# A selective scan and sixteen experts in one kernel: the fourth state block's input product moves to GpSimd

## The chip, the cores and the metric

One core of a Trainium2 chip runs the whole program. The metric is the device time in microseconds from launch to end, and of several executions the median is given. The core has five engines with queues of their own: TensorE (PE; its weight loads are shown as PEld), VectorE (DVE), ScalarE (ACT), GpSimd (POOL) and SyncE (SP), which here only issues DMAs. They wait for one another by counting semaphores.

## The reference, cut to what matters

8 sequences of 1024 tokens, 256 features, all in fp32. A Mamba layer stands between layer norms, and behind it a layer of 16 experts, of which each token uses 4. Only the scan matters for the change:

```python
dt = softplus(dt @ dt_proj_w + dt_proj_b)            # tokens x 512 channels
dA = exp(dt[..., None] * A)                          # x 16 states
dBx = dt[..., None] * Bm[:, :, None, :] * xc[..., None]
h = dA_t * h + dBx_t                                 # along the tokens
y_t = einsum('bds,bs->bd', h, C_t)
y = (y + xc * D) * silu(z) @ out_proj_w + residual
# then layer norm, routing, and for each token
y = sum over experts of weight * (silu(g) * u) @ down_proj
```

## The kernel before

The 8192 tokens are cut into 16 chunks of 512 (`CH`), two to a sequence. A chunk with an odd number carries its first states on from the chunk before (`carry`), an even one starts from zero. 512 channels times 16 states are 64 rows of 128 partitions for each chunk; four such rows are a group, so a chunk has 16 groups (`GPC`) and the program 256 (`NGRP`). A group is one third of the ring `hs` (`NH = 3`), a tile of 128 partitions by four state blocks (`NBETA`, `beta`) of 512 tokens.

A pass p of the schedule has 16 turns g, one for each group G = 16 p + g of chunk p. In the same turns TensorE and ScalarE prepare chunk p + 1 (the projections, the convolution, z, dt: the functions `f_...`), chunk p − 1 is closed and routed (`p_...`), and the experts of the chunk before run, one expert each turn, ten turns late (`MOFF`). Passes 0 and the greater part of 1 have no expert work. In pass 15 no next chunk is left. Each engine's program is written by hand as a loop over all turns, and its order in a turn is the order of the calls; nothing reorders it.

What happens to a group:

- VectorE forms dx times B for group G + 1 at the end of turn G (`inputs`, line 858): one instruction over all four blocks, 2048 columns. It waits for the loads of dx and B and, by `s_y`, for TensorE to be done with group G − 2, which used the same third of the ring.
- ScalarE forms exp(A dt) block by block into two PSUM banks (`decay`, line 501), waiting for the scan before the last.
- VectorE scans the four blocks in turn G (`scan`, line 872), each from its decays in PSUM and its inputs in `hs`. Around the first scan stand two products for an expert (lines 987 and 992).
- GpSimd waits until VectorE has formed the inputs of group G (`s_u`), weighs one expert's activations (`weigh`, line 751), and multiplies group G − 1 by C, all 2048 columns in one instruction (`read_out`, line 761).
- TensorE sums group G − 2 over its states into the bank Y (`add_states`, line 446) as the first thing of its turn G, then multiplies the expert's gate and up weights (416, 424), then the projections of that turn (343, 353, 379 and others), then the down weights of an older expert (434).
- VectorE multiplies Y by silu(z) in every fourth turn (`y_out`, line 879).

Between the fourth scan and the inputs VectorE has the work of a particular turn: the convolution's taps in turns 2 and 3 (line 831), Newton steps for the norms in turns 4, 6 and 12 (lines 788 to 817, opened by `tensor_scalar` at 801 or 810), the routing in turn 9 (924 to 983), the product for dx in turn 10 (847), residual sums in turns 5 and 13 (891, 1003). SyncE issues every load; those of dx and B wait by `s_u` until their buffer's last reader is done.

Of the kernel before, what the change touches and what calls it, by code (L numbers as in the profile page):

```python
# [6 lines left out]
ALU = mybir.AluOpType  # L7
ACT = mybir.ActivationFunctionType
AX = mybir.AxisListType
P = 128  # L10
# [3 lines left out]
CH = 512  # L14
TB = CH // P
KM = DM // P
MT = DI // P
# [4 lines left out]
NSIG = NS // SG  # L22
NBETA = P // CB
GPC = MT * NSIG
NGRP = NC * GPC
HIST = TAPS - 1
NH, NTH, NWD = (3, 3, 4)
# [43 lines left out]
def sandwich_kernel(nc, x, w_in, w_out, w_gu, w_dn, w_x, w_rt, cols, alog, ebias, consts, sel_dt, out):  # L71
    with ExitStack() as ctx:

        def sb(name, shape, dt=F32):
            return ctx.enter_context(nc.sbuf_tensor(name, shape, dt))
# [4 lines left out]
        def sem(name):  # L80
            return ctx.enter_context(nc.semaphore(name))
# [53 lines left out]
        dxr = sb('dxr', [P, 2, NBETA, CH])  # L135
        Bb = sb('Bb', [P, NSIG, CH])
        Cb = sb('Cb', [P, NSIG, CH])
        hs = sb('hs', [P, NH, NBETA, CH])
# [25 lines left out]
        f_act = Steps(sem('f_act'), ['xT0', 'xT1', 'raw0', 'tap0', 'raw1', 'tap1', 'raw2', 'tap2', 'raw3', 'tap3', 'z0', 'silu_x', 'xd', 'dt', 'z1', 'z2', 'z3', 'silu_z'])  # L164
        f_dve = Steps(sem('f_dve'), [f'c{k}{m}' for m in DVE_CONV for k in range(HIST)] + ['hist', 'dx'])
        fp_full = sem('fp_full')
        s_u, s_dA, s_h, s_keep, s_c, s_y, y_gate = (sem(k) for k in ('s_u', 's_dA', 's_h', 's_keep', 's_c', 's_y', 'y_gate'))
        route = ['den', 'score', 'sfc', 'ps', 't1', 't2', 'gs', 'ggt', 'geq', 'gq', 'ga', 'gr', 'gm', 'tmp', 'top', 'gt', 'eq', 'ng', 'cs', 'cn', 'ok', 'sel', 'w', 'ws', 'we', 'wr', 'comb']
        p_dve = Steps(sem('p_dve'), ['w1', 'nb', 'x1', 'Bw1'] + rsqrt_names('q') + ['Bnb'] + route)
        p_act = Steps(sem('p_act'), ['xn0', 'xn1', 'rev0', 'rev1', 'nm', 'sq', 'ro', 'sum2', 'nm2', 'sq2', 'x2', 'x2T0', 'x2T1', 'sig', 'cmT'])  # L170
# [7 lines left out]
        ld_dx = [sem(f'ld_dx{k}') for k in range(4)]  # L178
        ld_B = [sem(f'ld_B{s}') for s in range(NSIG)]
# [12 lines left out]
        def expert_at(G):  # L192
            q = G - GPC - MOFF
            return q if 0 <= q < NC * NE else None

        def groups():
            for p in range(-2, NC + 2):
                for g in range(GPC):
                    yield (p, g, p * GPC + g)

        @block.sync
        def _(sp):
# [18 lines left out]
            def load_dx(M, k):  # L221
                if M % MT == 0:
                    sp.wait_ge(st_dx, 16 * (M // MT + 1))
                if M >= 2:
                    sp.wait_ge(s_u, (M - 1) * NSIG)
                src = dx_d.rearrange('(M c k b) t -> M k c (b t)', k=2, b=2, c=CB)[M, k]
                sp.dma_start(dxr[:, M % 2, 2 * k:2 * k + 2, :].rearrange('p b t -> p (b t)'), src.unsqueeze(1).broadcast_to([CB, SG, 2 * CH])).then_inc(ld_dx[2 * (M % 2) + k], 16)

            def load_B(c, s):
                if s == 0:  # L230
                    sp.wait_ge(st_xd, 16 * (c + 1))
                if c > 0:
                    sp.wait_ge(s_u, c * GPC - NSIG + s + 1)
                src = bc_d.rearrange('(c k s g) t -> c k s g t', c=NC, k=2, s=NSIG)[c, 0, s]
                sp.dma_start(Bb[:, s, :], src.unsqueeze(0).broadcast_to([CB, SG, CH])).then_inc(ld_B[s], 16)

# [18 lines left out]
            for p, g, G in groups():  # L255
                c = p + 1
# [19 lines left out]
                if 0 <= p < NC:  # L276
                    M = p * MT
                    if g in (4, 8):
                        load_dt(M + g // NSIG + 1)
                        load_dx(M + g // NSIG + 1, 0)  # L280
                        load_dx(M + g // NSIG + 1, 1)
                    if g in (0, 1):
                        load_C(p, g + 2)
                if in_f(p) and g >= 12:
                    load_B(c, g - 12)
# [5 lines left out]
                if in_f(p) and g == 13:  # L291
                    load_dt(c * MT)
                    load_dx(c * MT, 0)
                    load_dx(c * MT, 1)
# [450 lines left out]
        @block.gpsimd  # L745
        def _(pool):

            def weigh(q):
                pool.wait_ge(m_w, q + 1)
                pool.wait_ge(ld_cm[q % 2], 16 * (q // 2 + 1))  # L750
                pool.tensor_tensor(th[:, q % NTH, :], th[:, q % NTH, :], cmb[:, q % 2, :], ALU.mult).then_inc(m_a, 1)  # L751

            def read_out(G):
                c, m, s = (G // GPC, G // NSIG % MT, G % NSIG)
                if m == 0:
                    pool.wait_ge(ld_C[s], 16 * (c + 1))
                if c % HALVES < HALVES - 1:
                    pool.wait_ge(s_keep, c // HALVES * GPC + G % GPC + 1)
                else:
                    pool.wait_ge(s_h, (G + 1) * NBETA)  # L760
                pool.tensor_tensor(hs[:, G % NH, :, :], hs[:, G % NH, :, :], Cb[:, s, :].unsqueeze(1).broadcast_to([P, NBETA, CH]), ALU.mult).then_inc(s_c, 1)  # L761
            for p, g, G in groups():
                if 0 <= G < NGRP:
                    pool.wait_ge(s_u, G + 1)
                q = expert_at(G - 2)
                if q is not None:
                    weigh(q)
                if 0 <= G - 1 < NGRP:
                    read_out(G - 1)

        @block.vector
        def _(dve):
# [76 lines left out]
            def inputs(G):  # L849
                c, M, s = (G // GPC, G // NSIG, G % NSIG)  # L850
                if s == 0:
                    for k in range(2):
                        dve.wait_ge(ld_dx[2 * (M % 2) + k], 16 * (M // 2 + 1))
                if M % MT == 0:
                    dve.wait_ge(ld_B[s], 16 * (c + 1))
                if G >= NH:
                    dve.wait_ge(s_y, G - NH + 1)
                dve.tensor_tensor(hs[:, G % NH, :, :], dxr[:, M % 2, :, :], Bb[:, s, :].unsqueeze(1).broadcast_to([P, NBETA, CH]), ALU.mult).then_inc(s_u, 1)  # L858

            def scan(G, beta):  # L860
                c, h = (G // GPC, G * NBETA + beta)
                k = G % GPC * NBETA + beta
                if beta == 0:
                    dve.wait_ge(s_u, G + 1)
                first = 0.0
                if c % HALVES:
                    if beta == 0:
                        dve.wait_ge(s_keep, c // HALVES * GPC + G % GPC + 1)
                    first = carry[:, k:k + 1]
                dve.wait_ge(s_dA, h + 1)  # L870
                hv = hs[:, G % NH, beta, :]
                dve.tensor_tensor_scan(hv, dA[h % 2][:, :], hv, first, ALU.mult, ALU.add).then_inc(s_h, 1)  # L872
# [131 lines left out]
            for p, g, G in groups():  # L1004
# [5 lines left out]
                if S:  # L1010
                    scan(G, 0)
                if q is not None:
                    expert_up(q)
                if S:
                    for beta in range(1, NBETA):
                        scan(G, beta)
# [35 lines left out]
                if 0 <= G + 1 < NGRP:  # L1052
                    inputs(G + 1)
# [34 lines left out]
```

## Time and profile before

| | |
|---|---|
| median of 3 runs | 2793.53 us (2791.71 to 2795.12) |
| the profiled execution | its span is 2792.0 us, and no time of its own beside it is given |
| VectorE busy | 2455.6 us, 88% of the span |
| TensorE busy (matmul) | 2414.2 us, 86% |
| ScalarE busy | 1628.2 us, 58% |
| GpSimd busy | 1474.8 us, 53% |
| DMA | 121 GB/s on the mean |
| mean granted TensorE clock | 0.953 of full speed |

The busy shares say how full an engine is over the whole span, not whether it sets the end. In the chain that ended last, TensorE has 42% of the span and VectorE 39%. A row of the timeline is one instruction, or a few like ones merged (xN), with start, duration, engine, line, output and inputs, and in brackets how long the engine stood idle before it and what released it. A matmul's end is modelled; GpSimd's times are rough.

### The profile page before, as it was taken

To read this page: it belongs to the slowest core of one execution; us is meant where nothing else is said; L and a number is where in the kernel's file an instruction comes from. 1 tells how busy PE (TensorE), PEld (TensorE's weight loads), DVE (VectorE), ACT (ScalarE), POOL (GpSimd) and SP (SyncE) were. 2 spreads that over 40 slices of the span, in tenths; PEclk is the share of its full clock that TensorE was granted. 3 is DMA by queue.
4 is the path that set the end of the run, shared out by engine and by line. 5 is a ranking of instruction groups with operands and counts; after the bars stand their busy time and mean duration, and the time that the engine had idled before them with its cause. 6 is when DMAs were issued, how large, how long until landed. Compare 5 with 4: busy or idle time off the path is not lost.

```text
span 2792.0 us, 27042 instructions
## 1 busy us (share of the span) xinstructions
PE 2414.2 (86%) x8416; PEld 1179.1 (42%) x8416; DVE 2455.6 (88%) x3265; ACT 1628.2 (58%) x3312; POOL 1474.8 (53%) x516
## 2 busy tenths in 40 slices
PE   4556799898989989899998989899898989988898
PEld 1112254443534444354444435354444445444454
DVE  1799998989899998989989898999989899899642
ACT  3566565666666566665666656665666665654331
POOL 0355564646556564655555465565646556565511
PEclk9677899999999999999999999999999999999999
DMA  1532332425244252524435252433525233352221
GB/s 36 226 107 90 129 139 96 160 94 177 77 144 140 98 170 81 188 74 143 133 105 172 79 184 83 136 130 105 179 79 175 95 124 128 100 177 70 64 76 59
DMA packets 164811, 336.65 MB, mean 121 GB/s; under 512 B 15771, under 2 KB 73404, under 8 KB 156220
## 3 DMA queue, kind: packets, MB, share of 16 engines
q1 hardware_dynamic: 164668, 334.93, 35.8%
q8 instruction: 67, 1.10, 0.2%
q14 instruction: 76, 0.62, 0.1%
HBM read 291.35 MB, written 43.52 MB: 120 GB/s over the span
## 4 chain that ended last, share of the span: by engine, by line
PE 42%; DVE 39%; issue 10%; ACT 9%; DMA 0%; SPq 0%; DVEq 0%; ACTq 0%
DVE hs L872 17%; DVE hs L858 9%; PE Gp L416 8%; PE Up L424 7%; PE MY L434 7%; PE FP L343 5%; PE FP L353 4%; PE FP L379 3%; PE Y L446 3%; DVE th L987 3%; DVE th L992 3%; PE FP L361 1%; ACT XC L571 1%; ACT XB L519 1%; ACT DX L636 1%
## 5 line engine op out<-in xcount | busy, mean ns | idle before, releaser
L761 POOL TENSOR_TENSOR hs<-hs,Cb 128x2048 f32<-128x2048 f32 x256 | 1159.1, 4528 | 203.7 <-DVE hs L858 203.7
L501 ACT ACTIVATE dA<-dtr,A 128x512 f32<-128x512 f32 x1024 | 699.7, 689 | 771.3 <-DVE hs L872 768.7
L751 POOL TENSOR_TENSOR th<-th,cmb 128x512 f32<-128x512 f32 x256 | 325.4, 1271 | 1096.8 <-DVE hs L858 980.7
L872 DVE TENSOR_TENSOR_SCAN hs<-dA,carry,hs 128x512 f32<-128x512 f32 x512 | 627.2, 1264 | 31.7 <-ACT dA L501 31.4
L416 PE MATMUL Gp<-x2T,Wgu 128*128 128x512 f32 x1024 | 530.4, 642 | 129.2 <-DVE th L987 129.0
L872 DVE TENSOR_TENSOR_SCAN hs<-dA,hs 128x512 f32<-128x512 f32 x512 | 596.2, 1203 | 50.6 <-ACT dA L501 50.1
L858 DVE TENSOR_TENSOR hs<-dxr,Bb 128x2048 f32<-128x2048 f32 x256 | 586.6, 2292 | 13.4 <-DMA dxr<-dx_d 12.3
L434 PE MATMUL MY<-Wdn,th 128*128 128x256 f32 x2048 | 486.3, 380 | 0.0
L424 PE MATMUL Up<-x2T,Wgu 128*128 128x512 f32 x1024 | 486.2, 597 | 0.0
L434 PEld LDWEIGHTS MY<-Wdn,th 128*128 128x128 f32 x2048 | 383.6, 190 | 136.5 <-issue 84.6
L416 PEld LDWEIGHTS Gp<-x2T,Wgu 128*128 128x128 f32 x1024 | 183.6, 198 | 473.4 <-issue 259.1
L446 PE MATMUL Y<-hs,Cst 128*32 128x512 f32 x2048 | 291.0, 642 | 21.5 <-POOL hs L761 21.5
L343 PE MATMUL FP<-xT,Win 128*128 128x512 f32 x512 | 262.1, 636 | 49.6 <-ACT SZ L565 15.8
L424 PEld LDWEIGHTS Up<-x2T,Wgu 128*128 128x128 f32 x1024 | 190.7, 192 | 260.8 <-issue 208.4
L987 DVE SCALAR_TENSOR_TENSOR th<-th,Gp 128x512 f32<-128x512 f32 x256 | 173.5, 678 | 68.1 <-ACT th L507 68.1
L507 ACT ACTIVATE th<-Gp 128x512 f32<-128x512 f32 x256 | 149.0, 582 | 114.8 <-PE Gp L416 114.8
L992 DVE TENSOR_TENSOR th<-Up,th 128x512 f32<-128x512 f32 x256 | 170.0, 664 | 10.0 <-PE Up L424 9.3
L343 PEld LDWEIGHTS FP<-xT,Win 128*128 128x128 f32 x512 | 95.8, 199 | 193.9 <-issue 94.5
L353 PE MATMUL FP<-XB,Kdiag 128*128 128x512 f32 x256 | 121.6, 620 | 11.6 <-ACT XB L551 11.6
L379 PE MATMUL FP<-Wout,SZ 128*128 128x256 f32 x512 | 122.6, 383 | 3.1 <-ACT DX L611 3.1
L379 PEld LDWEIGHTS FP<-Wout,SZ 128*128 128x128 f32 x512 | 98.0, 192 | 31.2 <-issue 14.3
L446 PEld LDWEIGHTS Y<-hs,Cst 128*32 128x32 f32 x2048 | 41.2, 110 | 149.5 <-issue 109.0
(131 smaller groups left out, 1827.1 us busy)
## 6 DMA issues: line engine op xcount, KB each, us to landing
dtr<-dt_d SPq DMA_DIRECT2D x64, 1024.0 KB, 5.5
dxr<-dx_d SPq DMA_DIRECT2D x128, 512.0 KB, 7.2
cmb<-cm_d SPq DMA_DIRECT2D x256, 256.0 KB, 3.6
Wdn<-in_w_dn SPq DMA_DIRECT2D x256, 128.0 KB, 3.5
dt_d<-XB SPq DMA_DIRECT2D x16, 1024.0 KB, 4.3
dx_d<-DX SPq DMA_DIRECT2D x16, 1024.0 KB, 5.8
Bb<-bc_d SPq DMA_DIRECT2D x64, 256.0 KB, 3.1
Cb<-bc_d SPq DMA_DIRECT2D x64, 256.0 KB, 4.0
```

Source lines behind the costliest of these rows:

```text
L343: mm = pe.matmul(FP[:, :], Win[:, q, c0:c0 + P], xT[:, q, :], start=q == 0, stop=q == KM - 1)
L379: pe.matmul(o, SZ[:, c % 2, m, b * P:(b + 1) * P], Wout[:, m, :], start=m == 0, stop=False)
L416: mm = pe.matmul(Gp[:, :], Wgu[:, k, e, 0:DE], x2T[:, c % 2, k, :], start=k == 0, stop=k == KM - 1)
L424: mm = pe.matmul(Up[:, :], Wgu[:, k, e, DE:2 * DE], x2T[:, c % 2, k, :], start=k == 0, stop=k == KM - 1)
L434: mm = pe.matmul(MY[b // 2][:, (b % 2) * DM:(b % 2 + 1) * DM], th[:, q % NTH, b * P:(b + 1) * P], Wdn[:, q % NWD, :], start=e == 0 and b % ...
L446: mm = pe.matmul(Y[beta * CB:(beta + 1) * CB, :], sel_y, hs[:, G % NH, beta, :], start=False, stop=s == NSIG - 1, tile_position=(0, beta * ...
L501: act.activation(dA[h % 2][:, :], dtr[:, M % 2, beta, :], ACT.Exp, scale=A[:, k:k + 1]).then_inc(s_dA, 1)
L751: pool.tensor_tensor(th[:, q % NTH, :], th[:, q % NTH, :], cmb[:, q % 2, :], ALU.mult).then_inc(m_a, 1)
L761: pool.tensor_tensor(hs[:, G % NH, :, :], hs[:, G % NH, :, :], Cb[:, s, :].unsqueeze(1).broadcast_to([P, NBETA, CH]), ALU.mult).then_inc(s ...
L858: dve.tensor_tensor(hs[:, G % NH, :, :], dxr[:, M % 2, :, :], Bb[:, s, :].unsqueeze(1).broadcast_to([P, NBETA, CH]), ALU.mult).then_inc(s_ ...
L872: dve.tensor_tensor_scan(hv, dA[h % 2][:, :], hv, first, ALU.mult, ALU.add).then_inc(s_h, 1)
L987: dve.scalar_tensor_tensor(out=th[:, q % NTH, :], in0=th[:, q % NTH, :], scalar=1.0, in1=Gp[:, :], op0=ALU.add, op1=ALU.mult).then_inc(m_v, 1)
```

## The change

GpSimd forms the input product of the fourth block (`last_input`), 512 columns, and VectorE's `inputs` keeps the other three, 1536 columns. GpSimd's product stands between `weigh` and `read_out` of a turn and is that of group G + 1. It carries its own semaphore, `s_u3`: the fourth scan waits for it, and SyncE's loads of dx and B wait for both counts.

```diff
@@ SyncE: load_dx and load_B
                     sp.wait_ge(s_u, (M - 1) * NSIG)
+                    sp.wait_ge(s_u3, (M - 1) * NSIG)
...
                     sp.wait_ge(s_u, c * GPC - NSIG + s + 1)
+                    sp.wait_ge(s_u3, c * GPC - NSIG + s + 1)
@@ GpSimd
+            def last_input(G):
+                c, M, s = (G // GPC, G // NSIG, G % NSIG)
+                if s == 0:
+                    pool.wait_ge(ld_dx[2 * (M % 2) + 1], 16 * (M // 2 + 1))
+                if M % MT == 0:
+                    pool.wait_ge(ld_B[s], 16 * (c + 1))
+                if G >= NH:
+                    pool.wait_ge(s_y, G - NH + 1)
+                pool.tensor_tensor(hs[:, G % NH, NBETA - 1, :], dxr[:, M % 2, NBETA - 1, :], Bb[:, s, :], ALU.mult).then_inc(s_u3, 1)
...
                 if q is not None:
                     weigh(q)
+                if 0 <= G + 1 < NGRP:
+                    last_input(G + 1)
                 if 0 <= G - 1 < NGRP:
                     read_out(G - 1)
@@ VectorE: inputs
-                dve.tensor_tensor(hs[:, G % NH, :, :], dxr[:, M % 2, :, :], Bb[:, s, :].unsqueeze(1).broadcast_to([P, NBETA, CH]), ALU.mult).then_inc(s_u, 1)
+                dve.tensor_tensor(hs[:, G % NH, 0:NBETA - 1, :], dxr[:, M % 2, 0:NBETA - 1, :], Bb[:, s, :].unsqueeze(1).broadcast_to([P, NBETA - 1, CH]), ALU.mult).then_inc(s_u, 1)
@@ VectorE: scan
+                if beta == NBETA - 1:
+                    dve.wait_ge(s_u3, G + 1)
```

GpSimd's queue in the middle of the program, before (three turns; `th` are an expert's activations, `cmb` its weights, `hs` the states):

```order
L751 TENSOR_TENSOR th<-th,cmb 128x512 [waits ld_cm0,m_w,s_u]
L761 TENSOR_TENSOR hs<-hs,Cb 128x2048 [waits s_keep]
L751 TENSOR_TENSOR th<-th,cmb 128x512 [waits ld_cm1,m_w,s_u]
L761 TENSOR_TENSOR hs<-hs,Cb 128x2048 [waits s_keep]
L751 TENSOR_TENSOR th<-th,cmb 128x512 [waits ld_cm0,m_w,s_u]
```

And now (`dxr` is dx, `Bb` is B):

```order
L753 TENSOR_TENSOR th<-th,cmb 128x512 [waits ld_cm0,m_w,s_u]
L763 TENSOR_TENSOR hs<-dxr,Bb 128x512 [waits s_y]
L773 TENSOR_TENSOR hs<-hs,Cb 128x2048 [waits s_h]
L753 TENSOR_TENSOR th<-th,cmb 128x512 [waits ld_cm1,m_w,s_u]
L763 TENSOR_TENSOR hs<-dxr,Bb 128x512 [waits s_y,ld_B0,ld_dx1]
L773 TENSOR_TENSOR hs<-hs,Cb 128x2048 [waits s_h]
```

A third instruction stands in each turn, with a wait for TensorE (`s_y`) in front of the read-out. VectorE's queue in turn 2 of a pass, before:

```order
L987 SCALAR_TENSOR_TENSOR th<-th,Gp 128x512 [waits m_th]
L872 SCALAR_TENSOR_TENSOR hs<-dA0,carry,hs 128x512 [waits s_dA,s_keep,s_u]
L992 TENSOR_TENSOR th<-Up,th 128x512 [waits m_v,m_u]
L872 SCALAR_TENSOR_TENSOR hs<-dA1,carry,hs 128x512 [waits s_dA]
L872 SCALAR_TENSOR_TENSOR hs<-dA0,carry,hs 128x512 [waits s_dA]
L872 SCALAR_TENSOR_TENSOR hs<-dA1,carry,hs 128x512 [waits s_dA]
L831 SCALAR_TENSOR_TENSOR XC<-XB,Cols,XC 128x512 [waits f_dve,f_act]
L831 SCALAR_TENSOR_TENSOR XC<-XB,Cols,XC 128x512 [waits f_dve] x2
L858 TENSOR_TENSOR hs<-dxr,Bb 128x2048 [waits s_y,ld_B3]
```

And the same turn now, from its third scan on:

```order
L888 SCALAR_TENSOR_TENSOR hs<-dA0,carry,hs 128x512 [waits s_dA]
L888 SCALAR_TENSOR_TENSOR hs<-dA1,carry,hs 128x512 [waits s_dA,s_u3]
L845 SCALAR_TENSOR_TENSOR XC<-XB,Cols,XC 128x512 [waits f_dve,f_act]
L845 SCALAR_TENSOR_TENSOR XC<-XB,Cols,XC 128x512 [waits f_dve] x2
L872 TENSOR_TENSOR hs<-dxr,Bb 128x1536 [waits s_y,ld_B3]
```

No instruction of VectorE changes its place; the last one is shorter and the fourth scan has one wait more.

## Rows read from the trace of the kernel before

**Rows 1.** The page's busy time: engine, us (share of the span), instructions.
```profile
PE 2414.2 (86%) x8416; PEld 1179.1 (42%) x8416; DVE 2455.6 (88%) x3265; ACT 1628.2 (58%) x3312; POOL 1474.8 (53%) x516
```

**Rows 2.** Timeline, VectorE and GpSimd in a short turn: start us, us, engine, line, operation.
```profile
1318.18 2.28 DVE L858 TENSOR_TENSOR hs<-dxr,Bb 128x2048 f32<-128x2048 f32 x1
...
1320.54 1.27 POOL L751 TENSOR_TENSOR th<-th,cmb 128x512 f32<-128x512 f32 x1 [4.08 <-DVE hs L858]
...
1321.76 4.52 POOL L761 TENSOR_TENSOR hs<-hs,Cb 128x2048 f32<-128x2048 f32 x1
...
1322.75 3.62 DVE L872 TENSOR_TENSOR_SCAN hs<-dA,carry,hs 128x512 f32<-128x512 f32 x3
...
1326.29 2.26 DVE L858 TENSOR_TENSOR hs<-dxr,Bb 128x2048 f32<-128x2048 f32 x1
```

**Rows 3.** Timeline, VectorE instructions alone and beside one of GpSimd.
```profile
1337.96 4.52 POOL L761 TENSOR_TENSOR hs<-hs,Cb 128x2048 f32<-128x2048 f32 x1
...
1342.25 2.38 DVE L858 TENSOR_TENSOR hs<-dxr,Bb 128x2048 f32<-128x2048 f32 x1
...
1554.66 1.21 DVE L891 TENSOR_TENSOR x<-DX,x 128x1024 f32<-128x1024 f32 x1
...
1699.01 4.54 POOL L761 TENSOR_TENSOR hs<-hs,Cb 128x2048 f32<-128x2048 f32 x1
...
1703.29 0.27 DVE L810 TENSOR_SCALAR ep_w<-e_s 128x4 f32<-128x4 f32 x1
...
2657.18 1.26 POOL L751 TENSOR_TENSOR th<-th,cmb 128x512 f32<-128x512 f32 x1 [9.59 <-DVE th L992]
2657.85 1.68 DVE L891 TENSOR_TENSOR x<-DX,x 128x1024 f32<-128x1024 f32 x1 [0.75 <-ACT DX L629]
```

**Rows 4.** Timeline of VectorE, the input products that open turns of pass 9.
```profile
1512.77 2.27 DVE L858 TENSOR_TENSOR hs<-dxr,Bb 128x2048 f32<-128x2048 f32 x1
...
1523.09 2.28 DVE L858 TENSOR_TENSOR hs<-dxr,Bb 128x2048 f32<-128x2048 f32 x1
...
1555.79 2.28 DVE L858 TENSOR_TENSOR hs<-dxr,Bb 128x2048 f32<-128x2048 f32 x1
...
1566.73 2.28 DVE L858 TENSOR_TENSOR hs<-dxr,Bb 128x2048 f32<-128x2048 f32 x1
...
1587.52 2.26 DVE L858 TENSOR_TENSOR hs<-dxr,Bb 128x2048 f32<-128x2048 f32 x1
...
1602.94 2.28 DVE L858 TENSOR_TENSOR hs<-dxr,Bb 128x2048 f32<-128x2048 f32 x1
```

**Rows 5.** Timeline of TensorE, the sums into Y in turns 2, 5, 6 and 9.
```profile
1517.48 1.07 PE L446 MATMUL Y<-hs,Cst 128*32 128x512 f32 x8
...
1550.33 1.06 PE L446 MATMUL Y<-hs,Cst 128*32 128x512 f32 x8
...
1562.69 1.06 PE L446 MATMUL Y<-hs,Cst 128*32 128x512 f32 x8
...
1594.96 1.06 PE L446 MATMUL Y<-hs,Cst 128*32 128x512 f32 x8
```

**Rows 6.** Timeline, VectorE in turn 7; ScalarE and TensorE in a turn 4.
```profile
1576.97 2.46 DVE L872 TENSOR_TENSOR_SCAN hs<-dA,carry,hs 128x512 f32<-128x512 f32 x2 [4.39 <-ACT dA L501]
...
1707.73 0.60 ACT L551 ACTIVATE XB<-FP 128x512 f32<-128x512 f32 x1 [0.62 <-PE FP L343]
...
1709.04 0.41 PEld L353 LDWEIGHTS FP<-XB,Kdiag 128*128 128x128 f32 x2
```

**Rows 7.** Timeline of TensorE in a turn 8, and its stretch (PEclk is the granted clock).
```profile
1421.37 3.18 PE L416 MATMUL Gp<-x2T,Wgu 128*128 128x512 f32 x4
...
1434.36 1.98 PE L416 MATMUL Gp<-x2T,Wgu 128*128 128x512 f32 x4
...
1420.00:1430.00 10.00, 10.00 (x25) 3.06 (x26) 10.00 (x11) 3.94 (x8) 7.78 (x4) 0.83 0.43 147
```

More of the change, by code:

```diff
@@ L166, in sandwich_kernel @@
         fp_full = sem('fp_full')
-        s_u, s_dA, s_h, s_keep, s_c, s_y, y_gate = (sem(k) for k in ('s_u', 's_dA', 's_h', 's_keep', 's_c', 's_y', 'y_gate'))
+        s_u, s_u3, s_dA, s_h, s_keep, s_c, s_y, y_gate = (sem(k) for k in ('s_u', 's_u3', 's_dA', 's_h', 's_keep', 's_c', 's_y', 'y_gate'))
         route = ['den', 'score', 'sfc', 'ps', 't1', 't2', 'gs', 'ggt', 'geq', 'gq', 'ga', 'gr', 'gm', 'tmp', 'top', 'gt', 'eq', 'ng', 'cs', 'cn', 'ok', 'sel', 'w', 'ws', 'we', 'wr', 'comb']
```

## The prediction

> **What bounds the kernel now.** I read three views in this order. The page's busy shares [rows 1]: VectorE 88% of the span (TensorE 86%), GpSimd 53%. So two engines are nearly full and the third looks free; the change takes from the first and gives to the third. The timeline of one short turn [rows 2] shows who stands when. I call t the end of VectorE's input product, which opens a turn (1318.18 + 2.28 = 1320.46). GpSimd weighs from t + 0.08, reads out from t + 1.30 and ends at t + 5.82 (1326.28). VectorE's last scan ends at t + 5.91 (1326.37), and its next input product takes it to 1328.55: the turn is 8.09 us. So GpSimd has no slack in such a turn: it ends in the very moment in which VectorE comes to the input product, and its idle time is that product alone. Last, the same timeline on VectorE and TensorE over one pass of 16 turns, where one sees which of the two is ahead [rows 4, 5]. (Half of the passes carry states on, half start from zero: odd and even ones.)
>
> **Part 1, a shorter input product.** It goes from 2048 to 1536 columns. Between 1.21 us for 1024 columns [rows 3] and 2.26 for 2048 [rows 2] a column costs 1.03 ns, so 512 columns are 0.53 us, 256 times: 134 us at most, if VectorE set the end everywhere.
>
> **Part 2, one more product on GpSimd, ahead of the read-out.** Weighing has the same shape and starts 1.22 us before the next instruction [rows 2], so the read-out starts and ends 1.22 us later: at t + 7.04. The order fence shows that nothing else moves on GpSimd. Nothing waits for the new product itself: the fourth scan that needs it comes a whole turn later.
>
> **Part 3, what the later read-out hits.** Pairs of rows tell it [rows 3]. VectorE's residual sum of 1024 columns, both inputs in SBUF, takes 1.21 us alone; begun at 2657.85 beside a GpSimd product that runs from 2657.18 to 2658.44, it takes 1.68 and ends 1.09 after GpSimd: of 0.59 us overlap it lost 0.47. A small tensor_scalar that begins 0.26 before a read-out ends (1703.55) ends at 1703.56 as well. The scans, with one input in PSUM, run beside read-outs throughout [rows 2]. So I take it that a VectorE instruction of the first kinds does nothing until the GpSimd instruction under way is done, but for the last 0.1 us. The trace shows overlaps up to 0.6 us only; the bounds for longer ones are nothing at all and the whole overlap, and I take the whole, since the rows lose four fifths of theirs. The Trainium skill (SBUF — State Buffer, section "Who interferes with whom") says the same of a VectorE instruction with two SBUF inputs against a GpSimd one that reads SBUF: an exclusive lock for the whole instruction, the later one fully blocked. By that rule the loss does not flatten for long overlaps; had it been shared bandwidth, the sum would be that of the third rival. The rows so far agree with the rule.
> Price in a short turn: the input product effectively starts at t + 7.0 and ends at t + 8.66, against t + 8.09: +0.57 with carried states. In a pass from zero the scans are 0.24 shorter in all, the read-out (1337.96 + 4.52) outlasts them already, and the input product takes 2.38 instead of 2.26 [rows 3]; with t 1.31 ahead of the read-out as in [rows 2] that turn is 7.98 (to 1344.63), and it becomes the same 8.66: +0.68. Where a conv tap, the product for dx or the routing stands behind the scans, the same wait falls on it: +1.0 − 0.53, +0.5 to +0.6. Where the gate of y (one PSUM input) stands first, its 0.58 covers the wait: about 0 and +0.2. Where VectorE waits for ScalarE anyway, −0.53.
>
> **Part 4, an added wait of GpSimd on TensorE.** The new product of turn G + 1 needs the buffer that group G − 2 leaves (s_y), and GpSimd asks for it at t + 1.30, where VectorE asked at the end of the turn. TensorE sums group G − 2 in turn G, and in the first half of a pass it runs behind. Turn 2 of the pass of [rows 4, 5] (counted from 0), t = 1515.04: the sum ends at 1518.55, t + 3.5. Turn 6, t = 1558.07: 1563.75, t + 5.7. Turn 9, t = 1589.78: 1596.02, t + 6.2. Behind the waiting product stands the read-out, and behind that, by part 3, VectorE. With the wait, read-out ends 5.85 us after the sum of Y (0.1 for the signal, 1.22 for the new product, 4.53).
> Laid along one carried pass (shift against before in brackets; what shifts VectorE shifts t):
> - 0 and 1: +0.57, then about 0 because of the gate of y (+0.5).
> - 2 (conv tap): Y at 1518.55, read-out ends 1524.40, conv and inputs end 3.72 later (the turn's 10.33, less 5.91 to the last scan, 0.53, and 0.17 of overlap) at 1528.12, where before it was 1525.37 (+2.7). 3 (conv tap): +0.5 (+3.2); TensorE's lag is used up.
> - 4: the wait for ScalarE's squares moves with VectorE, −0.53 (+2.7). But ScalarE's copy to XB, in line behind its decays, had 0.62 us of slack and TensorE's conv behind it 0.7 [rows 6]: 3.2 less 1.3 makes TensorE 2.0 late.
> - 5: Y ends 1551.39 + 2.0, read-out 1559.2, turn 1561.9 (+3.9). 6: Y 1563.75 + 2.0, read-out 1571.6, then the Newton steps of 2.4 and the inputs: 1575.7 against 1569.01 (+6.7).
> - 7: the 4.39 us wait for decays [rows 6], set by TensorE's and ScalarE's chain, which is 2 late, takes it back: +2.7. 8: TensorE again later than t + 1.30 by 0.7: +4.1.
> - 9 (routing): t = 1593.9; TensorE's sum 1596.02 + 2.2 = 1598.2; read-out 1604.1; routing and inputs 8.9 more (15.44 − 5.91 − 0.53 − 0.1): 1613.0 against 1605.22 (+7.8).
> - 10 to 15: VectorE sets each: +0.5, +0.57, −0.17 (part of z's wait covers it), −0.1, +0.57, +0.57: +9.7.
> The same walk over a pass that starts from zero states gives +10.6, since its short turns lose 0.68 and the routing turn begins later against Y. The last pass has no next chunk on TensorE, so only turns 3 and 4 wait: +7.2. The two passes without experts: there no weighing hides the first 1.2 us of TensorE's lag; by the same steps, with more of it taken back in ScalarE's waits, +18 for both together, the softest term.
> Sum: 7 × 10.6 + 6 × 9.7 + 7.2 + 18 = 158 us. Span 2792.0 + 158 = 2950, and 1.5 outside it (median of the runs 2793.5 less this span): 2951.
> The added waits of the DMA queue cost nothing: GpSimd's product of a turn is done before VectorE's of the same turn, so s_u stays the last of the two. What it needs (dx, B) it needs some 6 us earlier; those loads go out two or more turns ahead. Bounds of the new product itself: 1.22 from weighing, at most 1.27.
>
> **Rivals.**
> 1. The lock holds, but the wait on Y is absorbed: TensorE, less pressed, catches up by as much. Then part 3 alone: +2.5 a carried pass, +3.3 the others, +4.7 the last, +5 the first two: 6 × 2.5 + 7 × 3.3 + 9.7 = 48, 2841. For it: later turns of VectorE ease TensorE. Against it: TensorE runs its matmuls without a gap from turn 1 to turn 6, so Y's times in turns 2 and 6 don't get earlier.
> 2. TensorE, which now waits for VectorE in turns 10 to 15 and at turn 7, drops to 1.2 GHz more often. In turn 8 it already does so: the granted clock of ten microseconds is 0.83 (partly the lower level of 1.2 GHz), and the same four gate matmuls take 3.18 there, 1.98 a turn later [rows 7]. One more half turn of 10 us at that clock per pass, in a place where GpSimd waits for Y, is +5: 14 × 5 = 70, 3021.
> 3. The other side: no blocking beyond the short overlaps seen. VectorE then starts its input product at t + 5.83 and keeps the 0.53 in the eight turns of the second half and one of the first (the rest are TensorE's): −4.7 a pass, −66, and −12 in the first two: 2715. It decides if a read-out that overlaps by over 1 us stretches the product by less than 0.5. Against it stand all rows of the overlap.
> 4. Both effects cancel: the loss per short turn is near 0.5 and Y's wait small: 2793 ± 5.
>
> **How the numbers follow.** Forecast 0.63, rival 1 0.14, rival 2 0.13, rival 3 0.07, rival 4 0.03. Forecast alone 2890 to 2990 (the first-pass term and the 2 us that TensorE loses are the soft ones). The range takes in rival 1 and half of rival 2: 2835 to 3010. A measurement of this kernel tells 0.2% from no change; faster 0.07, same 0.03, slower 0.90.
>
> **What would show it.** In a short turn: read-out ends at t + 7.0, the input product lasts about 2.8 to 3.0 us by the profile instead of 1.74, and ends 1.6 after the read-out; turn 8.66. In turns 2, 6 and 9: GpSimd idle on TensorE's Y, 2 to 4 us each, and the first conv tap, the first Newton step and the routing's first step stretched by as much. VectorE busy time goes up, not down, since blocked time counts as busy. Wrong if the 1536-column product takes 1.75 us while a read-out runs beside it, or if no GpSimd wait on Y shows in turns 6 and 9.

## The result and the profile after

The changed kernel takes 2975.98 us (median of 4 runs, 2973.58 to 2978.44) against 2793.22 (2791.71 to 2795.12): a ratio of 1.0654, 95% interval 1.0639 to 1.0669. The profiled execution has a span of 2971.8 us, 179.8 more than before.

The page's busy time of the changed kernel answers to [rows 1]:

```profile
PE 2456.7 (83%) x8416; PEld 1187.2 (40%) x8416; DVE 2738.4 (92%) x3265; ACT 1632.9 (55%) x3312; POOL 1791.0 (60%) x772
```

VectorE was given less to do and is busy for 283 us more. The groups that are costliest, out of the same page (busy us, mean ns of one, idle time before it and its releaser), say where:

```profile
L773 POOL TENSOR_TENSOR hs<-hs,Cb 128x2048 f32<-128x2048 f32 x256 | 1157.9, 4523 | 0.0
...
L872 DVE TENSOR_TENSOR hs<-dxr,Bb 128x1536 f32<-128x1536 f32 x256 | 586.7, 2292 | 12.4 <-DMA dxr<-dx_d 12.4
L763 POOL TENSOR_TENSOR hs<-dxr,Bb 128x512 f32<-128x512 f32 x256 | 325.1, 1270 | 336.8 <-PE Y L448 188.0
...
L845 DVE SCALAR_TENSOR_TENSOR XC<-XB,Cols,XC 128x512 f32<-128x512 f32 x96 | 143.9, 1499 | 14.3 <-ACT XC L557 12.0
```

The product over 1536 columns has the mean that the one over 2048 had (2292 ns), by chance: 143 of the 256 take about 1.75 us, where no GpSimd instruction runs beside them, and the 113 that began more than 0.3 us before the end of one all end 1.61 or 1.62 us behind that end, whether they had overlapped it for 0.6 us or for 3.5. The conv taps went from 753 to 1499 ns. GpSimd's own instructions kept their length. Its new one waited for TensorE's Y for 188 us.

A short turn of the changed kernel in the timeline, which answers to [rows 2] (start us, us, engine, line):

```profile
1599.61 3.06 DVE L872 TENSOR_TENSOR hs<-dxr,Bb 128x1536 f32<-128x1536 f32 x1
...
1602.75 1.27 POOL L753 TENSOR_TENSOR th<-th,cmb 128x512 f32<-128x512 f32 x1 [1.69 <-DVE hs L872]
...
1603.97 1.27 POOL L763 TENSOR_TENSOR hs<-dxr,Bb 128x512 f32<-128x512 f32 x1
...
1604.97 3.62 DVE L888 TENSOR_TENSOR_SCAN hs<-dA,carry,hs 128x512 f32<-128x512 f32 x3
1605.20 4.51 POOL L773 TENSOR_TENSOR hs<-hs,Cb 128x2048 f32<-128x2048 f32 x1
1608.51 2.82 DVE L872 TENSOR_TENSOR hs<-dxr,Bb 128x1536 f32<-128x1536 f32 x1
```

With t = 1602.67 the read-out ends at t + 7.04 (1609.71), the product is shown from t + 5.84 to t + 8.66 (1611.33), 1.62 after the read-out. The turn was 8.09.

Turn 9 of pass 9, in which the routing begins, shows what answers to [rows 3] and the last of [rows 5]:

```profile
1698.33 1.27 POOL L753 TENSOR_TENSOR th<-th,cmb 128x512 f32<-128x512 f32 x1 [1.70 <-DVE hs L872]
...
1701.61 1.06 PE L448 MATMUL Y<-hs,Cst 128*32 128x512 f32 x8
...
1702.79 1.26 POOL L763 TENSOR_TENSOR hs<-dxr,Bb 128x512 f32<-128x512 f32 x1 [3.19 <-PE Y L448]
1704.01 4.50 POOL L773 TENSOR_TENSOR hs<-hs,Cb 128x2048 f32<-128x2048 f32 x1
1704.08 4.48 DVE L940 TENSOR_SCALAR DX<-DX 128x64 f32<-128x64 f32 x1
...
1715.12 0.68 DVE L895 TENSOR_TENSOR SZ<-Y,SZ 128x512 f32<-128x512 f32 x1
1715.72 1.75 DVE L872 TENSOR_TENSOR hs<-dxr,Bb 128x1536 f32<-128x1536 f32 x1
...
1715.86 2.08 PE L445 MATMUL Y<-XC,Ddiag 128*128 128x512 f32 x2 [6.58 <-DVE SZ L895]
...
1717.87 1.94 PE L448 MATMUL Y<-hs,Cst 128*32 128x512 f32 x8
...
1719.92 1.26 POOL L763 TENSOR_TENSOR hs<-dxr,Bb 128x512 f32<-128x512 f32 x1 [1.09 <-DVE th L1008]
```

A tensor_scalar over 64 columns, 0.17 us in the kernel before, stands for 4.48 us, from the start of the read-out to its end (1708.51 and 1708.56). The row at 1715.72 is the product alone, 1.75 us; its end is t of turn 10 (1717.47). The last three rows belong to turn 10: TensorE can't begin Y before VectorE's gate of the old Y, which stands behind the whole routing, and GpSimd's new product waits for that Y to t + 2.45 (the row's releaser is wrong here, Y ends at 1719.81 and frees it).

Between the ends of the input products of both traces one gets what each turn gained or lost:

| turn | 0 | 1 | 2 | 3 | 4 | 5 | 6 | 7 | 8 | 9 | 10 | 11 | 12 | 13 | 14 | 15 | pass |
|---|---|---|---|---|---|---|---|---|---|---|---|---|---|---|---|---|---|
| carried (pass 9) | 0.56 | 0.0 | 2.9 | 0.5 | −0.55 | 1.2 | 2.75 | −3.9 | 0.57 | 3.8 | 1.7 | 0.57 | −0.17 | 0.0 | 0.57 | 0.57 | 11.05 |
| from zero (pass 8) | 0.68 | 0.24 | 3.0 | 0.7 | −0.53 | 1.5 | 2.0 | −3.9 | 0.72 | 2.6 | 1.7 | 0.69 | −0.05 | 0.23 | 0.69 | 0.68 | 10.91 |

Passes 0 and 1 lost 13.1 and 19.0, the last 8.9; the start came 3.5 earlier. (The start moves by some us from one profiled execution to the next: in that of the last experiment below it came 2.7 later.)

### The profile page after: what moved, and what is told of

The parts are those of the page before. It is cut to its first block, busy times and chain, and to the rows that moved or that the text cites. A ratio compares the mean times of both kernels' runs of the same rounds, so it can differ in the third digit from the quotient of the medians.

```text
span 2971.8 us, 27801 instructions
## 1 busy us (share of the span) xinstructions
PE 2456.7 (83%) x8416; PEld 1187.2 (40%) x8416; DVE 2738.4 (92%) x3265; ACT 1632.9 (55%) x3312; POOL 1791.0 (60%) x772
## 4 chain that ended last, share of the span: by engine, by line
DVE 68%; issue 21%; PE 7%; ACT 4%; POOL 0%; DVEq 0%; DMA 0%; SPq 0%; ACTq 0%; POOLq 0%
DVE hs L888 27%; DVE hs L872 13%; DVE th L1008 5%; DVE th L1003 5%; DVE XC L845 4%; DVE p_w L815 2%; PE MY L436 2%; PE Gp L418 2%; PE Up L426 1%; DVE DX L944 1%; ACT XB L521 1%; DVE DX L940 1%; DVE SZ L895 1%; PE FP L345 1%; DVE ep_w L824 1%
## 5 line engine op out<-in xcount | busy, mean ns | idle before, releaser
L418 PE MATMUL Gp<-x2T,Wgu 128*128 128x512 f32 x1024 | 550.8, 664 | 161.3 <-DVE th L1003 160.2
L872 DVE TENSOR_TENSOR hs<-dxr,Bb 128x1536 f32<-128x1536 f32 x256 | 586.7, 2292 | 12.4 <-DMA dxr<-dx_d 12.4
L763 POOL TENSOR_TENSOR hs<-dxr,Bb 128x512 f32<-128x512 f32 x256 | 325.1, 1270 | 336.8 <-PE Y L448 188.0
L426 PE MATMUL Up<-x2T,Wgu 128*128 128x512 f32 x1024 | 498.7, 610 | 0.0
L426 PEld LDWEIGHTS Up<-x2T,Wgu 128*128 128x128 f32 x1024 | 198.2, 200 | 277.6 <-issue 206.7
L345 PE MATMUL FP<-xT,Win 128*128 128x512 f32 x512 | 258.0, 628 | 45.4 <-ACT SZ L567 13.1
L445 PE MATMUL Y<-XC,Ddiag 128*128 128x512 f32 x128 | 84.0, 744 | 111.5 <-DVE SZ L895 111.5
L845 DVE SCALAR_TENSOR_TENSOR XC<-XB,Cols,XC 128x512 f32<-128x512 f32 x96 | 143.9, 1499 | 14.3 <-ACT XC L557 12.0
```

The costliest lines, as they stand in the source:

```text
L345: mm = pe.matmul(FP[:, :], Win[:, q, c0:c0 + P], xT[:, q, :], start=q == 0, stop=q == KM - 1)
L418: mm = pe.matmul(Gp[:, :], Wgu[:, k, e, 0:DE], x2T[:, c % 2, k, :], start=k == 0, stop=k == KM - 1)
L426: mm = pe.matmul(Up[:, :], Wgu[:, k, e, DE:2 * DE], x2T[:, c % 2, k, :], start=k == 0, stop=k == KM - 1)
L763: pool.tensor_tensor(hs[:, G % NH, NBETA - 1, :], dxr[:, M % 2, NBETA - 1, :], Bb[:, s, :], ALU.mult).then_inc(s_u3, 1)
L872: dve.tensor_tensor(hs[:, G % NH, 0:NBETA - 1, :], dxr[:, M % 2, 0:NBETA - 1, :], Bb[:, s, :].unsqueeze(1).broadcast_to([P, NBETA - 1, CH] ...
```

## The experiments

Each ratio is to the kernel before, run on the same chip; its median was 2793.2 beside the change and 2789.6, 2792.6 and 2791.5 beside the experiments, so times of different experiments compare to some 4 us. Line numbers in the rows are those of each kernel; 872 is the input product in those that contain the change.

### GpSimd's product in the turn in which it is used

```diff
-                if 0 <= G + 1 < NGRP:
-                    last_input(G + 1)
+                if 0 <= G < NGRP:
+                    last_input(G)
```

> The change with one difference: in turn G GpSimd forms the fourth block of group G, not of group G + 1, so its wait for TensorE's Y is long over. Theory A (a VectorE instruction with two SBUF inputs stands still until GpSimd's instruction is done, and the wait for Y does the rest): the wait's part goes, the later read-out stays. Short turns still 8.66 us, turns 2, 6, 9 and 10 lose their 2 to 3 us extra; about +3.3 a pass from zero, +2.5 a carried one, +4.7 the last, +5 the first two: 2841. Theory B (the wait for Y alone makes the kernel slow, and there is no standing still): VectorE keeps its 0.53 us, 2715 to 2793. Theory C (the wait for Y costs nothing, GpSimd's extra work all of it): as the change, 2976.

Measured: 2853.25 us, ratio 1.0217 (1.0196 to 1.0238). The page's row of VectorE's product:

```profile
L872 DVE TENSOR_TENSOR hs<-dxr,Bb 128x1536 f32<-128x1536 f32 x256 | 558.0, 2180 | 12.4 <-DMA dxr<-dx_d 12.3
```

So of the 183 us of the change about 120 hang on one wait, and 64 over its own kernel before are left with it gone. (`s_u3`, on which SyncE's loads wait too, comes later for a group here as well, but VectorE's wait for dx is 12.3 us as in the change, 12.4.) A short turn is 8.67 as in the change (+0.57 and +0.70), turns 2, 6 and 9 of a carried pass are +0.5, +0.2 and +0.6. Theories B and C fall. A pass lost 3.3 (carried) and 4.1 (from zero), 0.8 more than I had expected; turn 7 took back 1.2 to 1.5. Passes 0 and 1 lost 2.5 together.

### The same without the relief of VectorE

On top of the edit above:

```diff
-                dve.tensor_tensor(hs[:, G % NH, 0:NBETA - 1, :], dxr[:, M % 2, 0:NBETA - 1, :], ...)
+                dve.tensor_tensor(hs[:, G % NH, :, :], dxr[:, M % 2, :, :], ...)
```

> As e1_same_turn, but VectorE forms all four blocks as before the change, and GpSimd forms the fourth once more over the same values: the relief of VectorE is taken away, the later read-out stays. Theory A: each turn in which VectorE sets the end is 0.53 longer than in e1_same_turn, that is nine turns of a pass and nearly all of the last and of the first two: 14 x 4.8 + 8 + 15 = 90 over it, about 2930; a short turn 9.19. Theory B: the kernel before, 2793, plus next to nothing.

Measured: 2962.83, ratio 1.0615 (1.0599 to 1.0631). A short turn is 1.10 longer than before, +0.53 against the experiment above: the relief is real and is worth 110 us; the later read-out without it costs 173. The guess for the sum was 33 too low: in the passes with experts turns 1 to 6 kept all of the 0.53, so that a pass is 6.6 to 6.8 longer than in the experiment above, where I gave it 4.8; passes 0 and 1 measured 19 where I had 20.

### One SBUF input in place of two

```diff
-                dve.tensor_tensor(hs[:, G % NH, 0:NBETA - 1, :], dxr[...], Bb[...], ALU.mult).then_inc(s_u, 1)
+                dve.tensor_reduce(hs[:, G % NH, 0:NBETA - 1, :], dxr[:, M % 2, 0:NBETA - 1, :].unsqueeze(3), AX.X, ALU.add).then_inc(s_u, 1)
```

This too stands on top of the first edit. The factor B is left out of three of four blocks.

> As e1_same_turn, but VectorE's instruction over 1536 columns is a sum over one element each (it copies dx and leaves the factor B out of three blocks): same columns, one SBUF input in place of two, on the same engine at the same place, and the read-out beside it as before. Theory A in its strict form (only two SBUF inputs stand still): it runs 1.7 us beside the read-out, a short turn is 7.57; conv taps, Newton steps and routing still stand still; some 6 us a pass less than e1_same_turn, about 2755. If any VectorE instruction with its output in SBUF stands still, or if it is bandwidth that is short: as e1_same_turn.

Measured: 2756.12, ratio 0.9876 (0.9861 to 0.9891). The page's row of VectorE's operation that stands in for the product (busy us, mean ns of one, idle time before it):

```profile
L872 DVE TENSOR_REDUCE hs<-dxr 128x1536 f32<-128x1536 f32 x256 | 444.1, 1735 | 13.2 <-DMA dxr<-dx_d 12.5
```

And three rows of the timeline, GpSimd's read-out and what VectorE does beside it and behind it:

```profile
1503.18 4.52 POOL L773 TENSOR_TENSOR hs<-hs,Cb 128x2048 f32<-128x2048 f32 x1
1506.46 3.37 DVE L845 SCALAR_TENSOR_TENSOR XC<-XB,Cols,XC 128x512 f32<-128x512 f32 x3
1509.74 1.75 DVE L872 TENSOR_REDUCE hs<-dxr 128x1536 f32<-128x1536 f32 x1
```

The copy over the same 1536 columns takes 1.735 us on the mean and 1.753 at most, whatever GpSimd does, and short turns are 0.55 shorter than before (0.66 from zero). Conv taps, with two SBUF inputs, stand still as they did: three take 3.37 here against 2.29 in the kernel before. So the columns, the output and the turn don't decide it. The edit changes the inputs and the operation at once and can't part the two. What speaks for the inputs is the trace of the change, over all of VectorE's instructions that began more than 0.3 us before the end of a GpSimd one: every input product (113), conv tap (31), residual sum (31), product for dx (15) and sum of two SBUF inputs in the routing (8) was stretched, and none of the 770 scans, of the 213 expert products and gates with one input in PSUM, or of the 8 reciprocals with a single SBUF input. The exception is tensor_scalar, with a single one: all 59 were stretched. The copy also rules out that GpSimd's read-out takes so much of SBUF's bandwidth that anything beside it slows.

### GpSimd's product behind the read-out

```diff
-                if 0 <= G + 1 < NGRP:
-                    last_input(G + 1)
                 if 0 <= G - 1 < NGRP:
                     read_out(G - 1)
+                if 0 <= G + 1 < NGRP:
+                    last_input(G + 1)
```

> The change with GpSimd's product (of group G + 1) behind the read-out, not ahead of it. The read-out ends at t + 5.8 as in the kernel before, TensorE gets its group as early as before, the wait for Y is over by then but for turn 9 (t + 6.2). Theory A: the new product begins at t + 5.8, as VectorE comes to its input product at t + 5.83, and one of the two stands still: 1.2 us if GpSimd is first. Short turn 8.66, all about as e1_same_turn, 2835 to 2850. Theory B: 2715 to 2793.

Measured: 2814.24, ratio 1.0084 (1.0069 to 1.0099), 21 us below the lower end of what I expected. The timeline of two turns shows why:

```profile
1498.68 4.51 POOL L773 TENSOR_TENSOR hs<-hs,Cb 128x2048 f32<-128x2048 f32 x1
...
1501.96 2.85 DVE L872 TENSOR_TENSOR hs<-dxr,Bb 128x1536 f32<-128x1536 f32 x1
1503.15 2.79 POOL L763 TENSOR_TENSOR hs<-dxr,Bb 128x512 f32<-128x512 f32 x1
...
1505.90 1.26 POOL L753 TENSOR_TENSOR th<-th,cmb 128x512 f32<-128x512 f32 x1
```

VectorE came during the read-out and stood still to its end at 1503.19, then went first: its product ends at 1504.81, and GpSimd's, 1.27 us alone, stands for 2.79 and ends 1.13 after it. The standing still works both ways, and at the border between two GpSimd instructions the one that already waits gets its turn: 113 of GpSimd's 256 new products took over 2.5 us. Of the 1.5 us that GpSimd loses 1.0 shows in the next turn: its read-out ends at t + 6.83 in place of 5.83, and a short turn of that kind is 8.45 (+0.35 carried); a short turn behind one in which GpSimd lost nothing is 7.56 (−0.53, turns 8 and 14 of pass 9). In the short turns of the change and of the experiment that forms the product in its own turn, VectorE always comes in the middle of a 4.5 us instruction.

### Two ways to fill turn 7's wait

VectorE idles 4.4 us in turn 7 [rows 6]. First, GpSimd forms all four blocks there behind its read-out, and VectorE nothing:

```diff
+                if g == 7 and 2 <= p < NC - 1:
+                    pool_inputs(G + 1)          # 2048 columns, counts s_u
...
-                if 0 <= G + 1 < NGRP:
+                if 0 <= G + 1 < NGRP and not (g == 7 and 2 <= p < NC - 1):
                     inputs(G + 1)
```

> The kernel before, with the whole input product (2048 columns) of the group after turn 7 moved to GpSimd, behind its read-out, in passes 2 to 14 only. There VectorE stands 4.4 us waiting for ScalarE's decays, so GpSimd's instruction runs from t + 5.8 to t + 10.35 under that wait and VectorE's last scan ends at t + 10.42. Theory A: nothing of VectorE with two SBUF inputs falls into it but the small copy behind the scans; the turn loses its 2.2 us: 13 x 2.2 = 28, 2762. Theory B (GpSimd's extra work hurts wherever it stands): same or slower.

Second, VectorE forms them itself, but between its second and third scan:

```diff
+                ahead = g == 7 and 0 <= p < NC - 1
...
+                        if ahead and beta == 2:
+                            inputs(G + 1)
                         scan(G, beta)
...
-                if 0 <= G + 1 < NGRP:
+                if 0 <= G + 1 < NGRP and not ahead:
                     inputs(G + 1)
```

> The kernel before, with VectorE's own input product of turn 7 moved ahead, between the second and the third scan, where VectorE waits 4.4 us; nothing goes to GpSimd. Theory A: placed at t + 3.65 it stands still until the read-out ends at t + 5.8 and is done at t + 8.0, as the decays come (t + 7.96): 2.2 us less in 13 passes, 1.5 in the first two, 2760. Its row should read about 4.3 us instead of 2.28. Without standing still: the same time, and the row 2.28.

Measured: 2789.52, ratio 0.9992 (0.9983 to 1.0), and 2791.17, ratio 0.9999 (0.9991 to 1.0008). Both did in turn 7 what was expected, and neither gained. Timeline of the first, turns 7 and 8:

```profile
1574.00 4.51 POOL L759 TENSOR_TENSOR hs<-dxr,Bb 128x2048 f32<-128x2048 f32 x1
...
1576.13 2.46 DVE L882 TENSOR_TENSOR_SCAN hs<-dA,carry,hs 128x512 f32<-128x512 f32 x2 [4.38 <-ACT dA L501]
...
1579.25 0.58 ACT L507 ACTIVATE th<-Gp 128x512 f32<-128x512 f32 x1
...
1579.86 0.69 DVE L997 SCALAR_TENSOR_TENSOR th<-th,Gp 128x512 f32<-128x512 f32 x1 [1.21 <-ACT th L507]
```

VectorE's scans end at 1578.6 and the next thing it does is at 1579.86: of 2.2 us saved 1.2 became a wait for ScalarE's tanh, which stands behind four decays. The other 0.9 went in turns 8 and 9 (from the starts of the expert's first product: −0.9 in turn 7, +0.84 in turn 9), where VectorE waits 0.41 for decays and 0.21 for the routing's logits; the rest of the 0.84 I have not traced. In the second kernel, in which the 0.9 was kept in some passes (pass 9 is one) and given back in others, the row of the product reads 4.52 us, standing still beside the read-out as expected, and costs nothing, under the wait. So VectorE alone doesn't set the end of turns 7 to 9 in the kernel before; ScalarE or TensorE does. My theory had taken the one wait for the bound.

### What sets turns 7 to 9

```diff
                 if R_ and g == 6:
+                    p_x2(p)                     # ahead of f_z and f_silu of this turn
                 if F and g in (6, 11, 12):
                     f_z(p, {6: 0, 11: 2, 12: 3}[g])
...
-                if R_ and g == 6:
-                    p_x2(p)
```

> The kernel before, with one call of ScalarE moved: the four normalising rows for the routing (p_x2, 2.06 us) stand ahead of z's copy and the silu in turn 6, where ScalarE waits 2.84 us for TensorE. Nothing of the change is in it; it asks what sets turns 7 to 9, in which e5 and e6 gave their 2.2 us back (1.2 to the expert's tanh, 0.9 to the routing's logits). Theory D (ScalarE's chain of copy, silu, rows, decays, tanh and transposed copies sets turns 7 to 9): the whole chain comes 2.0 us earlier, and the pass is 2.0 shorter: 13 x 2.0 = 26, 2766. If TensorE or its clock sets them: the decays come earlier, and the time is given back in turn 8 or 9: 2785 to 2793.

> e5 (GpSimd forms the whole input product of turn 7 in passes 2 to 14) and e8 together. With the decays 2.0 us earlier VectorE's last scan ends at t + 8.4, GpSimd's product at t + 10.35 as before: it is then GpSimd that is late, by 1.9. Theory D: no better than e8 alone and some 0.3 a pass less good than it or better, since VectorE's own product would end at t + 10.6: 2762 to 2768. If turns 7 to 9 are TensorE's: as e8.

Measured: 2765.38, ratio 0.9902 (0.9887 to 0.9917), and with GpSimd's product of turn 7 besides 2761.33, ratio 0.9885 (0.9869 to 0.9902). ScalarE's row of turn 6 in the kernel before:

```profile
1569.14 0.60 ACT L565 ACTIVATE SZ<-FP 128x512 f32<-128x512 f32 x1 [2.84 <-PE FP L343]
```

ScalarE's rows of turn 6 and VectorE's scan of turn 7 in the first of the two:

```profile
1553.62 2.07 ACT L636 ACTIVATE DX<-x,p_nb,p_w 128x256 f32<-128x256 f32 x4 [0.55 <-DVE p_nb L804]
...
1555.91 0.60 ACT L565 ACTIVATE SZ<-FP 128x512 f32<-128x512 f32 x1 [0.22 <-PE FP L343]
...
1561.77 2.46 DVE L872 TENSOR_TENSOR_SCAN hs<-dA,carry,hs 128x512 f32<-128x512 f32 x2 [2.42 <-ACT dA L501]
```

ScalarE's wait for TensorE was 2.84 us and is 0.22, VectorE's was 4.39 and is 2.42, and the gain stays (2.0 a pass carried, 2.3 from zero): theory D held, at 2765 where 2766 was expected. Both kernels beat the one before, by 1.0 and 1.2%, and the changed one. The two intervals overlap, so what the second adds is not shown; it came out just below the expected 2762 to 2768.

### The gate of y ahead of the routing

In the changed kernel:

```diff
-                if g != 9 and G % NSIG == 1 and 0 <= G - 2 < NGRP:
+                if G % NSIG == 1 and 0 <= G - 2 < NGRP:
                     y_out(G - 2)
...
-                if g == 9 and 0 <= G - 2 < NGRP:
-                    y_out(G - 2)            # stood behind the routing
```

> The changed kernel with one call moved: in turn 9 the gate of y stands ahead of the routing, not behind it. In the changed kernel TensorE's Y of turn 10 waits for that gate, GpSimd's new product for Y (t + 2.4 instead of t + 1.3), VectorE for the read-out behind it. Theory A: turn 10 loses its extra 1.1 to 1.2, and the gate runs in the time in which the routing stands still, 0.58 more: 1.7 in 14 passes, 24 in all, 2952. If the extra of turn 10 has another cause: 2966 at best.

Measured: 2961.8, ratio to before 1.0607 (1.0591 to 1.0623), 14 less than the change where 24 were expected. Turn 10 lost its extra (0.57 and 0.70 in place of 1.7). The gate itself was covered in turn 9 of carried passes (3.2 in place of 3.8) and not in those from zero (2.8 against 2.6). Turn 9 of pass 8 shows why, first in the change, then here:

```profile
1531.13 0.16 DVE L940 TENSOR_SCALAR DX<-DX 128x64 f32<-128x64 f32 x1
1531.33 0.55 DVE L942 RECIPROCAL DX<-DX 128x64 f32<-128x64 f32 x1
1531.91 3.83 DVE L944 TENSOR_TENSOR DX<-DX,Ebias 128x64 f32<-128x64 f32 x1
```

```profile
1529.06 4.04 DVE L940 TENSOR_SCALAR DX<-DX 128x64 f32<-128x64 f32 x1
```

In the change the tensor_scalar slips in just before GpSimd's read-out, which runs from 1531.16 to 1535.67; the reciprocal runs beside it, and only the third instruction stands still. With the gate in front the first one already does.

The extra of turn 10 needs the gate behind the routing, but not that alone. In the experiment that forms the product in its own turn the gate stands at the same place of the turn (t − 2.35), and Y is done at t + 0.51, before GpSimd would ask for it at t + 1.30; in the change it is done at t + 2.34. TensorE in that experiment, and its stretch (us, busy time of PE, PEld, DVE, ACT and POOL, granted clock, DMA):

```profile
1632.97 1.13 PE L445 MATMUL Y<-XC,Ddiag 128*128 128x512 f32 x2 [0.41 <-DVE SZ L895]
1634.03 1.06 PE L448 MATMUL Y<-hs,Cst 128*32 128x512 f32 x8
...
1630.00:1635.00 5.00, 4.59 (x20) 1.89 (x18) 4.66 (x13) 4.07 (x5) 0.33 (x1) 1.00 0.12 46
```

And the stretch of turn 10 in the change, whose two TensorE rows are shown further up (2.08 and 1.94 us):

```profile
1715.00:1720.00 5.00, 4.14 (x11) 0.97 (x12) 5.00 (x7) 0.69 (x1) 1.36 (x2) 0.51 0.00 0
```

In the change TensorE has been idle for 6.58 us before these matmuls and the granted clock is 0.51, the lower of its two levels (1.2 GHz); in the experiment it had been idle for 0.41 us and the clock is 1.00. So the same ten matmuls take 1.8 us longer, and 1.1 of the turn's 1.7 us is GpSimd's wait for them. It is so in passes 2 to 14 alike (idle 5.8 to 6.6 us before, against 1.5 at most). Moving the gate takes away the idle time as well as the wait (the two matmuls ahead of Y take 1.02 there), so this last experiment can't part the two.

## Why the prediction was right, and where it was not

The time, 2976 against 2951 forecast, is in the range, and the mechanism is the forecast's. That it came so near is in part luck: turn 10 and the first two passes were put too low, turn 8 too high, and the mechanism of rival 2, which the forecast put at nothing, has a share.

- **A shorter product.** 0.53 us per turn; with the relief taken away the short turn is 0.53 longer. Right.
- **The read-out later by 1.22.** t + 7.04 was forecast and measured.
- **VectorE stands still beside GpSimd.** Short turn 8.66, forecast 8.66. From overlaps of up to 0.6 us I took the whole of longer ones, and the traces bear it out: the 4.48 us tensor_scalar is a whole one, and the 113 stretched products end at the same distance behind GpSimd however long they had overlapped. GpSimd's 2.79 shows the other direction: the later one waits, whichever engine it is on. The Trainium skill (SBUF — State Buffer, "Who interferes with whom") has a VectorE instruction with two SBUF inputs contend with a GpSimd one that reads SBUF, the second fully blocked; the traces agree. The same section has tensor_reduce never contending on this chip, and tensor_scalar contending when it is in a 2-port mode. The mean of 1.735 us agrees with the first; the 4.48 us fits the second, though no run shows the mode.
- **The wait for Y.** It is about 120 of 183 us. Rival 1, in which it costs nothing, would have been 2841; with the wait removed the kernel measured 2853. Turns 5, 6, 7 and 9 of a carried pass were forecast as +1.2, +2.8, −4.0 and +3.7 and measured +1.2, +2.75, −3.9 and +3.8.
- **The size, 25 us short** (22 of it in the span, 180 against 158). Three terms. Turn 10 was put at +0.5 and is +1.7: I had seen the wait for Y where TensorE runs behind, and not that in turn 10 Y stands behind VectorE's own gate, which the code puts behind the routing, and that TensorE, idle until then, forms it at the lower clock. The first two passes were put at 18 and lost 32, less 3.5 of an earlier start that is not the change's; with the wait for Y removed they lost 2.5, so the term is the wait's, but which of their turns I had wrong was not worked out. Turn 2 was +2.2 and is +2.9, since its Y comes 0.57 later against the start of the pass. TensorE's projection in turn 1 waits for ScalarE's copy xT, which stands in line behind decays and so behind VectorE's scans, and these come 0.57 later (rows of the change; in the kernel before the copy stands at the same place of the turn, t + 4.23):

```profile
1615.56 0.58 ACT L545 ACTIVATE xT<-FP 128x512 f32<-128x512 f32 x1
...
1616.28 1.96 PE L345 MATMUL FP<-xT,Win 128*128 128x512 f32 x4 [0.33 <-ACT xT L545]
```

  Against that turn 8 was put at +1.4 and is +0.6: GpSimd's new product did not wait there at all.
- **Rival 2, more time at 1.2 GHz.** Right in turn 10, where it is about 1.1 us of a pass, 14 us over passes 2 to 15, and not the +5 a pass that it put. The forecast had no term for it. The mean granted clock fell from 0.953 to 0.938, and over the whole program the same gate matmuls cost 664 ns a piece against 642, 20 us of TensorE's time; how much of that outside turn 10 moved the end no run tells.
- **Rival 3.** Fell with the first row of a short turn. Its number, 2715, isn't reached even by the one-input copy, since conv taps and routing still stand still.

## What to carry to other kernels

Before an elementwise product moves from VectorE to GpSimd, lay both queues side by side in one turn and look which of VectorE's instructions have two SBUF inputs. Here these and GpSimd's instructions did not run together but for the last 0.1 us, so the sum of both is a bound of its own, whatever the busy shares say. Here GpSimd's three take 6.96 us on end and leave 1.62 of VectorE's product behind them (8.66 with the step of 0.08); before, two took 5.74, and 2.26 stood behind (8.09). Ask of each wait of a moved step when it is asked, not only for what: the same condition that held at a turn's end was not yet true in six turns of sixteen (2, 4, 5, 6, 9 and 10) when GpSimd asked at its beginning. And a wait that stands out on one engine names no bound: 2.2 us taken out under it brought nothing (ratios 0.9992 and 0.9999), while moving one step of the chain behind it brought 26 us.

## What was not expected of the hardware

A float32 tensor_scalar with a single input in SBUF stood still beside GpSimd too (4.48 us for 64 columns, and 59 of 59 in the trace), while a tensor_reduce with a single one did not (1.735 us mean), nor a reciprocal over 64 columns (0.55 us beside a read-out). And at the border between two GpSimd instructions, which follow each other without a gap in the records, a VectorE instruction that already waits gets in: GpSimd's next one then took 2.79 us instead of 1.27. And the wait behind the gate in turn 10 cost twice: TensorE had stood idle for 6.58 us, its granted clock was then 0.51 where it was 1.00 after 0.41 us of idling, and GpSimd waited for the slower matmuls.
